# First layer's experts with the inner tiles turned: copied weights as the stationary operand, clipping read from PSUM by two engines, outputs in two banks

## The reference, cut to what matters

```python
logits = xf @ Wg.T
idx = jnp.argmax(logits, axis=-1)
for e in range(E):                      # E = 8
    m = (idx == e)[:, None].astype(xf.dtype)
    h = jax.nn.relu(xf @ W1[e] + b1[e])     # 128 -> 512
    out = out + m * (h @ W2[e] + b2[e])     # 512 -> 128
```

## Time and profile before

| | |
|---|---|
| Median of 3 runs | 808.08 us (807.72 to 810.06) |
| Profiled execution | 811.75 us, of which the span is 809.6 us |
| PE / DVE / ACT / POOL busy in the span | 83% / 62% / 40% / 39% |
| Experts' stage, first matmul to first late score | 101.99 to 178.27 us |

### The profile page before, as it was taken

The page is one execution under the profiler, slowest core; times in us unless marked ns, Lnnn a source line. Parts: engine busy times, 40 slices in busy tenths (PEclk is TensorE's granted clock), DMA queues, the critical chain, the costliest instruction groups (busy, mean ns, idle before and its releaser), DMA issues.

```text
span 809.6 us, 13528 instructions
## 1 busy us (share of the span) xinstructions
PE 675.9 (83%) x4448; PEld 417.0 (52%) x4449; DVE 503.7 (62%) x1196; ACT 326.3 (40%) x498; POOL 317.0 (39%) x339
## 2 busy tenths in 40 slices
PE   3784887877773799988799999999999998689996
PEld 1463656645443546655344444444444434668885
DVE  6563235443545258768777777777787743577776
ACT  0631321213355325545145555556555652222222
POOL 6427000003703333352166767676767674500000
PEclk9988899999878669989789999999999999779999
DMA  9501010100000000000000000000000000000000
GB/s 310 202 0 49 17 40 27 52 26 27 26 1 0 1 1 3 2 2 2 1 1 1 1 0 0 0 0 0 0 0 0 0 1 2 1 0 1 13 13 26
DMA packets 16585, 17.19 MB, mean 21 GB/s; under 512 B 1568, under 2 KB 15008, under 8 KB 16160
## 3 DMA queue, kind: packets, MB, share of 16 engines
q1 hardware_dynamic: 15520, 14.55, 5.3%
q0 software_dynamic: 1024, 2.10, 0.9%
HBM read 11.40 MB, written 5.24 MB: 21 GB/s over the span
## 4 chain that ended last, share of the span: by engine, by line
PE 64%; DVE 19%; issue 6%; ACT 5%; POOL 4%; DVEq 1%; DMA 1%; ACTq 0%
PE ps L1745 10%; PE ps L1723 8%; PE ps L1733 6%; DVE region L964 6%; PE ps L1859 4%; PE ps L1469 3%; PE ps L1542 3%; PE ps L1486 3%; PE ps L1531 2%; PE ps L1643 2%; PE ps L1850 2%; PE ps L1848 2%; PE ps L1849 2%; ACT region L1171 2%; DVE rmax L809 2%
## 5 line engine op out<-in xcount | busy, mean ns | idle before, releaser
L964 DVE TENSOR_REDUCE region<-ps 128x1 f32<-128x512 f32 x256 | 168.4, 686 | 60.9 <-PE ps L1723 60.8
L1305 ACT ACTIVATE region<-ps 128x1024 f32<-128x1024 f32 x128 | 127.1, 1021 | 93.2 <-PE ps L1733 93.2
L1723 PE MATMUL ps<-kr,qmr 96*128 96x512 f32 x256 | 116.2, 461 | 16.5 <-DVE region L964 12.8
L680 POOL TENSOR_TENSOR region<-region 128x512 f32<-128x512 f32 x80 | 106.9, 1338 | 52.8 <-ACT region L1305 51.3
L1733 PE MATMUL ps<-qmr,kr 98*128 98x512 f32 x256 | 110.3, 439 | 3.1 <-ACT region L1305 2.3
L685 POOL TENSOR_TENSOR region<-region 128x512 f32<-128x512 f32 x64 | 82.1, 1283 | 39.2 <-ACT region L1305 34.5
L1745 PE MATMUL ps<-region 128*32 128x512 f32 x512 | 92.0, 599 | 0.1
L1752 PE MATMUL ps<-region,ones 128*32 128x512 f32 x192 | 92.1, 599 | 0.0
L1723 PEld LDWEIGHTS ps<-kr,qmr 96*128 96x128 f32 x256 | 49.7, 195 | 66.1 <-DVE region L964 63.3
L1486 PE MATMUL ps<-region 128*128 128x128 f32 x272 | 43.3, 311 | 40.1 <-ACT region L1181 30.2
L1733 PEld LDWEIGHTS ps<-qmr,kr 98*128 98x128 f32 x256 | 48.8, 193 | 48.7 <-issue 39.7
(11 more groups left out here) (264 smaller groups left out, 1209.9 us busy)
## 6 DMA issues: line engine op xcount, KB each, us to landing
region<-in_w SPq DMA_DIRECT2D x2, 2048.0 KB, 12.9
slots_in<-zeros SPq DMA_DIRECT2D x1, 1536.0 KB, 9.5
region<-slots_in SPq DMA_DIRECT2D x6, 256.0 KB, 2.8
slots_out<-og SPq DMA_DIRECT2D x6, 256.0 KB, 2.4
e<-in_e SPq DMA_DIRECT2D x1, 1152.0 KB, 15.9
x<-in_x SPq DMA_DIRECT2D x4, 256.0 KB, 3.8
out<-y SPq DMA_DIRECT2D x4, 256.0 KB, 2.3
e<-in_e SPq DMA_DIRECT2D x1, 576.0 KB, 16.8
```

The source lines that it names most:

```text
L680: ins = pool.tensor_tensor(o, held(tiles[0]), held(tiles[1]), ALU.add)
L964: dve.tensor_reduce(mxp[:, u // HM, u % HM:u % HM + 1], bank(b), AX.X, ALU.max).then_inc(mx_read, 1)
L1305: act.activation(pm[:, k % HELD, :], ps[:, b:b + 2, :].rearrange("p b c -> p (b c)"), ACT.Exp, scale=SCM).then_inc(p_whole, 1)
L1723: pe.matmul(bank(4 + u % 2 if first else u % 2), qm[0:R_ROWS, parity, h * P:(h + 1) * P], kr[0:R_ROWS, c:c + 512], start=True, stop=True). ...
```

## The change

The first products are computed turned at once. For each block of 128 hidden values the stationary operand is now the block of W1, and the 128 turned tokens are what moves, so that the hidden values come out in the partitions. The sixteen transposes of L1525 and the four copies to `hb` in a group go. The stationary operand is read from the fixed buffer `w1s` (in the place of `hb`, four windows), into which ACT copies the four experts' `w1` for each group. DVE adds and clips windows 0 and 2 straight from banks 2 and 4, ACT windows 1 and 3 from banks 3 and 5. Products 0 and 1 go to bank 1, products 2 and 3 to bank 6, each pair with its own signal. The wait for `og_ready` moves on PE from ahead of the first products to behind three of them.

```diff
 # DVE, mix(i)
-                for b in range(GROUP):
-                    dve.wait_ge(h_turned, i * GROUP + b + 1)
+                for b in (0, 2):
+                    dve.wait_ge(h_done, i * GROUP + b + 1)
                     for c in range(FC0):
-                        ins = dve.tensor_scalar(hT[:, b, c * P:(c + 1) * P], bank(6 + b % 2)[:, c * P:(c + 1) * P],
+                        ins = dve.tensor_scalar(hT[:, b, c * P:(c + 1) * P], bank(2 + b)[:, c * P:(c + 1) * P],
                                                 b1_col[:, e[b], c:c + 1], 0.0, ALU.add, ALU.max)
-                    ins.then_inc(hT_ready, 1)
-                    if b == 1 and more:
-                        rows_turned(i + 1)
+                    ins.then_inc(even_ready, 1)
+                if more:
+                    rows_turned(i + 1)
                 if not first:
                     dve.wait_ge(og_stored, i * 16)
-                dve.wait_ge(o_done, i + 1)
                 for b in range(GROUP):
-                    dve.tensor_tensor(og[:, b, :], bank(1)[:, b * D:(b + 1) * D], b2_row[:, e[b], :], ALU.add).then_inc(og_ready, 1)
+                    if b % 2 == 0:
+                        dve.wait_ge(o_done, i * 2 + b // 2 + 1)
+                    dve.tensor_tensor(og[:, b, :], bank(1 + 5 * (b // 2))[:, b * D:(b + 1) * D], b2_row[:, e[b], :], ALU.add).then_inc(og_ready, 1)
 # ACT
-            with act.Fori(0, GROUPS) as i:
-                for b in range(GROUP):
-                    act.wait_ge(h_done, i * GROUP + b + 1)
-                    act.activation(hb[:, b, :], bank(2 + b), ACT.Copy).then_inc(hb_ready, 1)
+            def odd_windows(i, first=False):
+                e = window_experts(mybir.EngineType.Activation, i)
+                if not first:
+                    act.wait_ge(o_done, i * 2)
+                for b in (1, 3):
+                    act.wait_ge(h_done, i * GROUP + b + 1)
+                    for c in range(FC0):
+                        ins = act.activation(hT[:, b, c * P:(c + 1) * P], bank(2 + b)[:, c * P:(c + 1) * P], ACT.Relu,
+                                             bias=b1_col[:, e[b], c:c + 1])
+                    ins.then_inc(odd_ready, 1)
+
+            def weights_copied(i):
+                e = window_experts(mybir.EngineType.Activation, i)
+                for b in range(GROUP):
+                    act.activation(w1s[:, b, :], w1[:, e[b], :], ACT.Copy).then_inc(w1s_ready, 1)
...
+            weights_copied(0)
+            odd_windows(0, first=True)
+            with act.Fori(1, GROUPS) as i:
+                weights_copied(i)
+                odd_windows(i)
 # PE, mix(i)
+            def hidden_turned(i, b):
+                pe.wait_ge(w1s_ready, i * GROUP + b + 1)
                 for c in range(FC0):
-                    ins = pe.transpose(bank(6 + b % 2)[:, c * P:(c + 1) * P], hb[:, b, c * P:(c + 1) * P], ident[:, :])
-                ins.then_inc(h_turned, 1)
+                    ins = pe.matmul(bank(2 + b)[:, c * P:(c + 1) * P], w1s[:, b, c * P:(c + 1) * P], xgT[:, b, :],
+                                    start=True, stop=True)
+                ins.then_inc(h_done, 1)
...
                 pe.wait_ge(xgT_ready, i + 1)
+                for b in range(3):
+                    hidden_turned(i, b)
                 if not first:
                     pe.wait_ge(og_ready, i * GROUP)
-                for b in range(GROUP):
-                    pe.matmul(bank(2 + b), xgT[:, b, :], w1[:, e[b], :], start=True, stop=True).then_inc(h_done, 1)
-                turn_hidden(i, 0)
-                turn_hidden(i, 1)
+                second_products(i, 0, e)
+                hidden_turned(i, 3)
                 if more:
                     turn_window_rows(i + 1)
-                for b in range(GROUP):
-                    ins = second_products(i, b, e)
-                    if b + 2 < GROUP:
-                        turn_hidden(i, b + 2)
-                ins.then_inc(o_done, 1)
+                for b in range(1, GROUP):
+                    second_products(i, b, e)
```

More of the change, by code:

```diff
@@ L258, in bass_recurrent_two_layers @@
         xgT = region.take(GROUP, P)
-        hb = region.take(GROUP, F0)
+        w1s = region.take(GROUP, F0)
         hT = region.take(GROUP, F0)
@@ L347, in bass_recurrent_two_layers @@
         xg_loaded = sem("xg_loaded"); xg_turned = sem("xg_turned"); xgT_ready = sem("xgT_ready")
-        h_done = sem("h_done"); hb_ready = sem("hb_ready"); h_turned = sem("h_turned"); hT_ready = sem("hT_ready")
+        h_done = sem("h_done"); even_ready = sem("even_ready"); odd_ready = sem("odd_ready"); w1s_ready = sem("w1s_ready")
         o_done = sem("o_done"); og_ready = sem("og_ready"); og_stored = sem("og_stored")
@@ L1202, in _ @@
                     steps[stage](i)
-            with act.Fori(0, GROUPS) as i:
-                for b in range(GROUP):
-                    act.wait_ge(h_done, i * GROUP + b + 1)
-                    act.activation(hb[:, b, :], bank(2 + b), ACT.Copy).then_inc(hb_ready, 1)
-            act.wait_ge(o_done, GROUPS)
+            def odd_windows(i, first=False):
[10 more added lines that the diff above has]
+                e = window_experts(mybir.EngineType.Activation, i)
+                for b in range(GROUP):
+                    act.activation(w1s[:, b, :], w1[:, e[b], :], ACT.Copy).then_inc(w1s_ready, 1)
+            act.wait_ge(s_wexp, 64)
+            act.wait_ge(wexp_ready, 1)
+            weights_copied(0)
[3 more added lines that the diff above has]
+                odd_windows(i)
+            act.wait_ge(o_done, GROUPS * 2)
             def gate(g):
@@ L1518, in turn_window_rows @@
                 ins.then_inc(xg_turned, 1)
[L1520 to L1523, removed]
+            def hidden_turned(i, b):
+                pe.wait_ge(w1s_ready, i * GROUP + b + 1)
                 for c in range(FC0):
-                    ins = pe.transpose(bank(6 + b % 2)[:, c * P:(c + 1) * P], hb[:, b, c * P:(c + 1) * P], ident[:, :])
-                ins.then_inc(h_turned, 1)
+                    ins = pe.matmul(bank(2 + b)[:, c * P:(c + 1) * P], w1s[:, b, c * P:(c + 1) * P], xgT[:, b, :],
+                                    start=True, stop=True)
+                ins.then_inc(h_done, 1)
             def second_products(i, b, e):
-                pe.wait_ge(hT_ready, i * GROUP + b + 1)
+                if b % 2 == 0:
+                    pe.wait_ge(even_ready, i * 2 + b // 2 + 1)
+                else:
+                    pe.wait_ge(odd_ready, i * 2 + b // 2 + 1)
                 for c in range(FC0):
-                    ins = pe.matmul(bank(1)[:, b * D:(b + 1) * D], hT[:, b, c * P:(c + 1) * P], w2[:, e[b], c, :],
+                    ins = pe.matmul(bank(1 + 5 * (b // 2))[:, b * D:(b + 1) * D], hT[:, b, c * P:(c + 1) * P], w2[:, e[b], c, :],
                                     start=(c == 0), stop=(c == FC0 - 1))
-                return ins
+                if b % 2 == 1:
+                    ins.then_inc(o_done, 1)
             def mix(i, first=False, more=True):
```

## The result

| | before | changed |
|---|---|---|
| Median | 809.07 us (4 runs, 807.72 to 810.26) | 785.06 us (4 runs, 783.49 to 789.27) |
| Ratio, 95% interval | | 0.969 (0.965 to 0.973) |
| Profiled execution / span | 811.75 / 809.6 us | 783.49 / 781.8 us |
| Experts' stage, first product to first late score | 76.28 us | 47.79 us |

A forecast was written before the change was run, and what follows sets the result against it. PE was taken to bound the experts' stage: 7.76 us issue plus 0.6 loop turn make 8.36 a group instead of 12.44, the stage 51.64 instead of 76.28; 808.08 - 24.6 = 783.5 us, range 779.5 to 790.5.

The forecast's parts named there:

- What bounds a group: Experts' stage: a ring through PE; a group's 12.44 us is 9.59 of PE's issue and 2.86 of its waits.
- no weight load was charged for: PE's first products: 24 more weight loads a group lie under the passes and add 0, not 2.6 us.
- waits between the engines inside the groups: PE's waits of 0.72, 0.26 and 0.34 us within a group of the kernel before, all expected to go.
- at the heads: PE's 1.54 us wait at a group's start for og's additions to empty bank 1; most of it expected to go.
- The turn of the loop, 0.6 a group: PE between groups: loading the experts' numbers, two register operations and a semaphore leave a gap of 0.6 us.
- the lower gap of 0.33: Lower end of PE's gap between groups; it would give 1.35 us more gain, 782.1 us in all.
- The load of the rows, taken as 0: PE's wait for the next group's rows: 0 to 0.4 us a group, of which 0 was taken.
- ACT beside PE: ACT's four copies at 0.63 us and clips at 0.3 to 0.5 take at most 7.2 of 8.36 a group, under PE.
- DVE not late anywhere: DVE in the experts' stage loses eight of sixteen additions, 345 ns each, and delays nobody.
- The low clock kept in the sum: First group of the experts' stage: 1.69 us lost to the 1.2 GHz level, left in the forecast.
- first products 8.2 to 8.7 us apart: Sign that the forecast is right: distance on PE from one group's first products to the next group's.
- Behind the stage everything moves as one: Gather, late attention and all of layer 1 start earlier by the stage's whole gain, 24.6 us.

The follow-up runs named there:

- e6: Changed kernel with sixteen transposes of a constant, which nobody waits for, added at each group's end on PE; stage 57.33 us (55.60 without low clock).
- e2: Kernel before with only PE's wait for og_ready moved, from ahead of the first products to ahead of the second; stage 69.64 us.
- e5: Changed kernel with four loads of the experts' numbers on PE in a group, one for each window, instead of one; stage 51.71 us.
- e3: Changed kernel with SP issuing the load of a group's rows ahead of the store instead of behind it; stage 48.20 us (46.57 without low clock).
- e8: Changed kernel with all clips on DVE and none on ACT, which only copies weights; stage 47.83 us.
- e9: Kernel before, unaltered, run and traced a second time; stage 74.55 us, median 813.73 us.
- e4: Changed kernel with three added loads of the experts' numbers on PE, values unused, which never got into the program; stage 47.52 us.

## Why the prediction was right, and where its terms were off

*What bounds a group* held: PE's issue. e6 shows it, and the 0.11 of a pass whose weights are loaded for it alone is in every row of L1542 above (24 passes in 2.68). That no weight load was charged for was right, as the second products' row had said. The trace of the changed kernel has 186 to 193 ns for a load of L1542, and one starts every 0.11 while PE works. The Trainium skill (TensorE: Matmul & The Clock Gate, LDWEIGHTS (loading the stationary operand)) has a load cost its columns at 1.2 GHz, 107 ns for 128 of them. That is shorter than the 186 to 193 that the trace gives one load, and the trace decides; it is near the distance from one to the next. Neither length is added to the passes here.

*Where the gain comes from.* PE's issue in the stage fell from 6 x 9.59 - 0.44 = 57.1 to 6 x 7.56 - 0.44 = 44.9, by 12.2. Its waits fell from 74.55 - 57.1 = 17.4 to 2.8, by 14.6. More than half of the 26.8 is waiting that went, and only 4.9 of it is to be had by moving one wait (e2). In the prediction's terms 17.4 is 6 x 1.32 = 7.9 of waits between the engines inside the groups, 5 x 1.54 = 7.7 at the heads, and the end. No run takes the handoffs away without the transposes, so this split is argued from rows and not shown.

*The turn of the loop, 0.6 a group,* is the term that failed: 3.0 us that did not appear, and the lower gap of 0.33 that the prediction allowed did not appear either. The length of the turn was about right: in e2 the first product starts 0.5 to 0.6 behind the start of the load, in e5 0.5 to 0.7 behind that of the last. The overlap was wrong. The sum let the load start as the last product is issued; in the kernel before and in e2, where that product waits for its clip, it starts 0.1 behind to 0.4 ahead of that, and in the changed kernel 0.7 to 1.2 ahead, so that it runs underneath. That the missing wait is what gives the lead fits all these traces, but no run put such a wait into the changed kernel. e5 shows that the lead ends.

*The load of the rows, taken as 0,* costs more than that: e3 removes 1.15, some 0.3 in each of four groups, within the 0 to 0.4 that stood in the bounds. Together with the loop's turn the stage was forecast at 49.95 without the low clock and measured at 47.72, 2.2 less.

*ACT beside PE* held: a clip every 0.26 (four in 1.14, 0.37 the last), below the 0.3 to 0.5 allowed; copies 0.61. The first copy ended near 130.9, 1.3 ahead of need. *DVE not late anywhere* held but for the 0.15 us of window 0's clip in three groups; sixteen clips on it instead of eight change nothing (e8). *The low clock kept in the sum* stood on both sides of the gain and did it no harm, but the stage's 51.64 had 1.69 of it where the first traces of the changed kernel had none. Of the signs that the prediction named, one failed beside the clips: first products 8.2 to 8.7 us apart, where they are 7.7 to 8.2.

*Behind the stage everything moves as one* held in what is done, but not to the us. From the first late score to the end of the span, the same instructions took 631.3 and 630.7 in the two traces of before and 628.1 to 637.0 in the changed kernel and the experiments. Ahead of the stage there is scatter too: it began between 90.7 (e5) and 103.8 (e9). That isn't the change, since e2, with the old order of the products, began at 100.72 and the changed kernel at 100.40 and 100.57. In the first two traces the span fell by 27.8: 1.6 ahead of the stage and 28.5 in it, less 2.3 behind. So a stage gain of 26.8, 2.2 over the forecast, came with a median gain of 24.0 in one comparison and 29.0 in the other, and some of the nearness of 785.06 to 783.5 is luck.

Does the earlier start cost anything systematic? Take for each of the eleven comparisons the gain of the medians less the gain in the stage (without low clock, from 74.55): it lies between -2.8 and 6.0, 1.2 in the mean. The medians show no loss. Why the same instructions take 628 to 637 stays open; the granted clock behind the stage is 0.92 in both first traces.

## What to carry to other kernels

Count a change on the engine that bounds the stage as issue and as waits apart: turning a product so that its output is already in the layout of the next removes the transposes and, with them, two handoffs from the chain; here issue fell by 12.2 us and waits by 14.6. A cost that shows at a loop's head need not show in the next kernel: ask whether the instructions ahead of it wait, since an engine that has work queued ahead can load registers beneath it, as far as its lead goes (one load here, not four). When totals scatter by more than the question, compare the stage in the trace, and take a second trace of the kernel before, too.

## What the hardware showed beside that

A load of the experts' numbers into registers took 0.33 to 0.35 us on PE, four in a row lay 0.40 apart; on ACT it took 0.31, on DVE 0.34 to 0.35. Only the first on each engine took 0.50 to 0.60. How far PE's load began ahead of the last issue before it depended on what that was: 0.7 to 1.2 behind fp32 products without waits (0.5 to 0.9 in e3), 1.4 to 1.7 behind the sixteen transposes of e6, 0.1 behind to 0.4 ahead where the last product waited for a clip. An unused load of registers did not reach the program (e4). A clip with a column from a register-held address cost ACT no more than a fixed one: 368 ns, where the nearest fixed form had 367.
